# Banded attention: the row maxima enter the exponentials as a bias, GpSimd's queue in another order, one expert pair moved to the end

## The reference

```python
x = x + window_attention(group_norm(x))   # 8x8 windows shifted by 4, 8 heads, cosine scores + bias
t = tokens(x)
t = t + banded_attention(layer_norm(t))   # blocks of 128 tokens, 4 heads of 32 channels:
    # attn = q @ k.T * 32 ** -0.5 + band_mask   (0 where 0 <= i - j <= 32, else -inf)
    # out  = softmax(attn) @ v @ Wproj + bproj
t = t + moe(layer_norm(t))                # gate, top 2 of 8 experts, each 128 -> 256 (gelu) -> 128
```

## Time and profile before

| | us |
|---|---|
| median of 3 runs (range) | 3118.3 (3107.27 to 3126.27) |
| profiled execution, its time | 3125.42 |
| profiled execution, its span | 3123.6 |
| PE busy | 2461.7 |
| DVE busy | 2008.5 |
| POOL busy | 1893.4 |
| ACT busy | 1793.8 |

### The profile page before, as it was taken

The page is one execution under the profiler, slowest core; times in us unless marked ns, Lnnn a source line. Parts: engine busy times, 40 slices in busy tenths (PEclk is TensorE's granted clock), DMA queues, the critical chain, the costliest instruction groups (busy, mean ns, idle before and its releaser), DMA issues. The chain is left out here.

```text
span 3123.6 us, 73042 instructions
## 1 busy us (share of the span) xinstructions
PE 2461.7 (79%) x26418; PEld 1739.3 (56%) x26418; DVE 2008.5 (64%) x5670; ACT 1793.8 (57%) x3432; POOL 1893.4 (61%) x1569
## 2 busy tenths in 40 slices
PE   6898888888888888888888888888888888765550
PEld 3565556666655666656556566656556566543430
DVE  3688876767766777667666677677676776652110
ACT  3666676666566665666665666656665666542220
POOL 0224455676666666666666666766666666777565
PEclk8999998998898888988888889889888889877775
DMA  2011123333233333333333333333333323333542
GB/s 75 19 32 39 43 73 72 61 76 78 57 72 69 71 74 72 63 78 63 72 70 70 71 75 61 76 67 68 69 73 71 74 56 67 78 76 74 130 87 26
DMA packets 247796, 210.79 MB, mean 67 GB/s; under 512 B 35261, under 2 KB 204361, under 8 KB 247249
## 3 DMA queue, kind: packets, MB, share of 16 engines
q0 software_dynamic: 94144, 69.54, 15.8%
q1 hardware_dynamic: 153296, 136.58, 15.5%
HBM read 119.73 MB, written 90.77 MB: 67 GB/s over the span
## 5 line engine op out<-in xcount | busy, mean ns | idle before, releaser
L1159 POOL DMA_INDIRECT out_dram<-yo,back_to x540 | 854.9, 1583 | 488.6 <-PE bank_s L627 160.6
L1142 POOL DMA_INDIRECT x_sorted<-xn_c,place_i x512 | 512.4, 1001 | 271.9 <-issue 130.5
L1135 POOL TENSOR_TENSOR s_sb_a<-s_sb_a,mx_a 128x512 f32<-128x512 f32 x256 | 266.7, 1042 | 453.9 <-DVE mx_a L1518 452.5
L1510 DVE TENSOR_TENSOR s_sb_a<-bank_s,bias_a 128x512 f32<-128x512 f32 x256 | 176.2, 688 | 323.3 <-PE bank_s L627 239.1
L754 PE MATMUL bank_m<-xe,wk_e 128*128 128x512 f32 x468 | 253.8, 675 | 38.9 <-ACT hid L1017 21.5
L1135 POOL TENSOR_TENSOR s_sb_b<-s_sb_b,mx_b 128x512 f32<-128x512 f32 x256 | 268.4, 1048 | 9.5 <-DVE mx_b L1518 9.0
L761 PE MATMUL bank_m<-wk_e,hid 128*128 128x128 f32 x1872 | 257.6, 304 | 1.7 <-ACT hid L1017 1.7
L627 PE MATMUL bank_s<-kk_a,q_a 32*64 32x128 f32 x4096 | 126.2, 301 | 165.2 <-DVE st_c L1272 51.4
L986 ACT ACTIVATE p_sb_a<-s_sb_a 128x512 f32<-128x512 f32 x256 | 160.8, 628 | 166.4 <-POOL s_sb_a L1135 166.4
L761 PEld LDWEIGHTS bank_m<-wk_e,hid 128*128 128x128 f32 x1872 | 253.9, 222 | 3.5 <-issue 3.3
L981 ACT ACTIVATE pt_sb_b<-bank_to 128x512 f32<-128x512 f32 x256 | 152.6, 596 | 162.3 <-PE bank_to L688 161.8
(11 more groups left out here) (230 smaller groups left out, 5935.0 us busy)
## 6 DMA issues: line engine op xcount, KB each, us to landing
wk_e<-in_w_experts_dram SPq DMA_DIRECT2D x127, 321.0 KB, 3.1
xs<-x_sorted SPq DMA_DIRECT2D x127, 260.0 KB, 2.8
xin<-in_x_dram SPq DMA_DIRECT2D x128, 112.0 KB
x_res<-in_x_dram SPq DMA_DIRECT2D x256, 56.0 KB
out_dram<-t SPq DMA_DIRECT2D x256, 56.0 KB
out_dram<-yo,back_to POOLq DMA_INDIRECT x540
x_sorted<-xn_c,place_i POOLq DMA_INDIRECT x512
x_res<-in_x_dram SPq DMA_DIRECT2D x256, 8.0 KB
```

Source lines behind the costliest of these rows:

```text
L1135: pool.tensor_tensor(s[:, :, :], s[:, :, :], m[:, :, None].to_broadcast(shape), ALU.subtract).then_inc(s_sub[w], 1)
L1142: pool.indirect_dma_start(out=x_sorted.ap(), out_offset=bass.IndirectOffsetOnAxis(ap=place_i[:, d % 2, TILES * choice + t:TILES * choice + ...
L1159: pool.indirect_dma_start(out=out, out_offset=bass.IndirectOffsetOnAxis(ap=back_to[:, q % IDS, j:j + 1], axis=0), in_=yo[:, q % YO, j, :], ...
L1510: tt(s_sb[0][:, :, :].rearrange("p (r h) n -> p r (h n)", h=2), scores, bias_a[:, kind, :, :].rearrange("p (r h) n -> p r (h n)", h=2), AL ...
```

## The change

It has four parts.

1. **Banded maxima.** DVE computes mask minus scores, so the tile holds the negated scores (the masked places hold +1e30), and its row reduction is a minimum, which is the negated maximum. POOL's subtraction for b is gone. ACT takes exp(-tile + minimum) head by head: four instructions of 128x128, each with its column of `mx_s[1]` as bias; they wait for the minima and not for POOL. The factor 32 ** -0.5 moves into the copies of the queries (`banded_copy`).
2. **POOL's order.** In a step it is now the a subtraction, then the scatters of the step, then the add-backs, with none of the waits for the scores or for the b output. `BACK_AT` names steps only: the first pair's eight add-backs stand at 4, 4, 4, 4, 5, 6, 7, 8, the second's at 9 (four) and 10 (four).
3. **The last pass.** `FREE_PASSES = 1`: pass 34 takes no pair, so pair 56 (batch 29, groups 111 and 112) becomes the first of the tail, which has 12 pairs and not 11.
4. **Padding.** SP issues the padding writes ahead of the third load of the tail, without waiting for the scatters, and waits for them ahead of the first load of the last batch.

```diff
+FREE_PASSES = 1
-BACK_AT = (((4, 0), (4, 1), (4, 2), (4, 3), (5, 1), (5, 2), (6, 1), (6, 2)),
-           ((9, 0), (9, 1), (9, 2), (9, 3), (10, 1), (10, 2), (10, 3), (11, 1)))
+BACK_AT = ((4, 4, 4, 4, 5, 6, 7, 8), (9, 9, 9, 9, 10, 10, 10, 10))
...
-            last = i == PASSES - 1 and n == SLOTS_PER_PASS - 1
-            if i >= pairs[u].batch + (5 if n == 0 else 4) and not last:
+            if i >= pairs[u].batch + (5 if n == 0 else 4) and i < PASSES - FREE_PASSES:
...
             for n, u in enumerate(tail):
+                if n == 2:
+                    set_pads()
                 if pairs[u].batch == IMAGES - 1 and pairs[tail[n - 1]].batch != IMAGES - 1:
-                    set_pads()
+                    sp.wait_ge(pads_set, 16 * E)
                 load_pair(sp, u)
...
             def probs(w, n):
-                act.wait_ge(s_sub[w], n + 1)
+                act.wait_ge((s_sub[0], s_max[1])[w], n + 1)
                 steps_done(act, pt_ready[w], n)
-                func(flat(p_sb[w][:, :, :]), flat(s_sb[w][:, :, :]), ACT.Exp,
-                     scale=1.0 if w == 0 else float(DB) ** -0.5).then_inc(p_ready[w], 1)
+                if w == 0:
+                    func(flat(p_sb[0][:, :, :]), flat(s_sb[0][:, :, :]), ACT.Exp).then_inc(p_ready[0], 1)
+                else:
+                    for h in range(HB):
+                        last = func(p_sb[1][:, h, :], s_sb[1][:, h, :], ACT.Exp, scale=-1.0, bias=mx_s[1][:, h:h + 1])
+                    last.then_inc(p_ready[1], 1)
...
-                if tiled(n):
-                    pool.wait_ge(s_ready[0], n + 1)
-                moves(0)
                 if tiled(n):
                     below_max(0, n)
-                if tiled(nb):
-                    below_max(1, nb)
-                moves(1)
-                moves(2)
-                steps_done(pool, o_ready[1], nb)
-                moves(3)
+                if t >= 5 and on(d):
+                    for k in range(4):
+                        scatter(d, 4 * (t - 5) + k)
+                if t == 0 and on(d - 1):
+                    for k in range(12, TOP * TILES):
+                        scatter(d - 1, k)
+...
-                    tt(s_sb[1][:, :, :], scores,
-                       const("mask_b")[:, None, :].to_broadcast([P, HB, P]), ALU.add).then_inc(s_added[1], 1)
+                    tt(s_sb[1][:, :, :], const("mask_b")[:, None, :].to_broadcast([P, HB, P]), scores,
+                       ALU.subtract).then_inc(s_added[1], 1)
...
-                dve.tensor_reduce(mx_s[w][:], s_sb[w][:, :, :], AX_X, ALU.max).then_inc(s_max[w], 1)
+                dve.tensor_reduce(mx_s[w][:], s_sb[w][:, :, :], AX_X, (ALU.max, ALU.min)[w]).then_inc(s_max[w], 1)
```

More of the change, by code:

```diff
@@ L133, in shape_constants @@
     d = n[:, None] - n[None]
-    put("mask_b", np.where((d >= 0) & (d <= RADIUS), 0.0, MASKED))
+    put("mask_b", np.where((d >= 0) & (d <= RADIUS), 0.0, -MASKED))
     r = np.arange(-(WS - 1), WS, dtype=np.float32)
@@ L482, in set_pads @@
                 sp.wait_ge(totals_kept, 1)
-                for h in range(2):
-                    sp.wait_ge(scattered[h], 16 * TILES * IMAGES)
                 for e in range(E):
@@ L490, in set_pads @@
                     sp.dma_start(rows, here).then_inc(pads_set, 16)
-                sp.wait_ge(pads_set, 16 * E)
             def spill(c, h):
@@ L971, in tokens_copy, with banded_copy @@
                 func(xt_c[:, half(h)], S[2], ACT.Copy).then_inc(ln_c, 1)
-            def banded_copy(b, h, dst, src, made, kept, reader):
+            def banded_copy(b, h, dst, src, made, kept, reader, scale=1.0):
                 need_half(act, made, b, h, 1, 1)
                 need(act, reader, b - 1, TILES, 4 if h else 8)
-                func(dst[:, half(h)], src, ACT.Copy).then_inc(kept, 1)
+                func(dst[:, half(h)], src, ACT.Copy, scale=scale).then_inc(kept, 1)
             def probs_copy(w, n):
@@ L1068, in step @@
                 if t == 7 and on(b):
-                    banded_copy(b, 0, q_b, S[1], bq_ready, bq_sb, s_ready[1])
+                    banded_copy(b, 0, q_b, S[1], bq_ready, bq_sb, s_ready[1], float(DB) ** -0.5)
                 if t == 0 and on(d):
@@ L1079, in step @@
                 if t == 2 and on(b):
-                    banded_copy(b, 1, q_b, S[2], bq_ready, bq_sb, s_ready[1])
+                    banded_copy(b, 1, q_b, S[2], bq_ready, bq_sb, s_ready[1], float(DB) ** -0.5)
                 if t == 2 and on(a):
@@ L1165, in step @@
                 n, nb = TILES * i + t, TILES * i + t - LAG
[L1166 to L1172, removed]
-                                    if when == (t + TILES * (i - j), k):
-                                        add_back(u, m)
-                    if t >= 5 and on(d):
-                        scatter(d, 4 * (t - 5) + k)
-                    if t == 0 and on(d - 1):
-                        scatter(d - 1, 12 + k)
-                if tiled(n):
-                    pool.wait_ge(s_ready[0], n + 1)
-                moves(0)
                 if tiled(n):
                     below_max(0, n)
-                if tiled(nb):
-                    below_max(1, nb)
-                moves(1)
-                moves(2)
-                steps_done(pool, o_ready[1], nb)
-                moves(3)
+                if t >= 5 and on(d):
[4 more added lines that the diff above has]
+                        scatter(d - 1, k)
+                for j in (i - 1, i):
+                    for slot in range(SLOTS_PER_PASS):
+                        u = slots[j][slot] if 0 <= j < PASSES else None
+                        if u is not None:
+                            for m, when in enumerate(BACK_AT[slot][0:SUB * len(pairs[u].members)]):
+                                if when == t + TILES * (i - j):
+                                    add_back(u, m)
             for i in range(-1, PASSES):
```

## The result

The changed kernel takes 3151.19 us (median of 4 runs, 3141.21 to 3158.28) against 3116.59 us (4 runs) of the kernel before: a ratio of 1.0108, with an interval of 1.0066 to 1.0150. It is slower, by about 34 us or 1.1%. The forecast was 3107 us.

What follows compares the result with a forecast made beforehand. No engine was full (PE busy 79%); chains passing between engines set the time. From the median 3118.3 us, +11 in the full passes and -22 at the end gave 3107 us, range 3079 to 3147.

Steps and rivals of the forecast that it cites:

- The exponentials: ACT's b tile: four 128x128 pieces with bias instead of one 128x512, 0.61 us more in each of 256 tiles.
- the waits behind them: PE's waits for ACT's a copy at steps 0 and 3, to grow from 0.93 to about 1.5 us.
- The sum: Full passes: 0.61 + 0.61 + 0.13 - 0.9 = +0.45 us each, +11 us in 25; with -22 after them, -11.
- rival B: Steps 0 and 3: longer waits put PE at half clock in every pass, +35 us, 3142 us; chance 0.24.
- The forecast's own sign for this: Full passes: the forecast counts as wrong if their granted clock moves by 0.02.
- Steps 6 and 7: PE's waits there shrink: -1.4 us in one kind of pass, -0.35 in the other, mean -0.9 us a pass.
- DVE's lateness: Step 6: DVE's landing wait and 2.02 us copy shrink, DVE over 2 us earlier, step 7's scores no longer wait.
- rival C: Step 7: PE's gap shrinks and the slow stretch behind it in every second pass goes, -19 us, 3088; chance 0.20.
- The end: Last passes and tail: -10 us from an earlier tail start, -12 from add-backs covering loads, together -22 us.
- the stall: Tail, groups 113 to 115: 12.69 us of waiting for late results, to be covered by 39 us of add-backs.
- rival E: Last passes: the end gives nothing, as DVE's and PE's chain is as long as POOL's list, 3129; chance 0.07.
- D: All four pieces held behind the value copies, or dearer issues: +1.2 us a pass, +30 us, 3137; chance 0.07.

Runs made afterwards that it cites:

- e1_bias_only: The kernel before with part 1 alone (maxima as bias, no POOL subtraction for b): 3160.28 us, ratio 1.0129 to the kernel before.
- e5_filler: The changed kernel with four unused 128x128 matmuls on PE ahead of the b transpose in steps 3 and 0: 3022.73 us, ratio 0.9687 to the kernel before.
- e3_order_and_end: The changed kernel without part 1 (POOL subtracts for b again, one exponential of 128x512): 3047.10 us, ratio 0.9762 to the kernel before.
- e4_copy_first: The changed kernel with ACT's a copy moved ahead of the inverse sums in steps 2 and 7: 3018.55 us, ratio 0.9678 to the kernel before.
- e8_one_bias_copy_first: The changed kernel with one minimum and bias per row, and the a copy ahead of the inverse sums in steps 2 and 7: 2992.87 us, ratio 0.9594.

## Why the prediction was wrong

**The exponentials** were priced right: +0.61 us a tile forecast, 0.65 measured. So were the waits behind them ("about 1.5 us"; 1.51 and 1.57 as means).

**What stands behind a longer wait** was the step that failed. The sum took the two waits at their length, 1.2 us a pass, "at the same clock", and set the clock aside as rival B with a chance of 0.24. Rival B is what happened, at the two places that it named. Before, the product behind the wait had taken 3.74 us in one pass and 5.13 in the other; after, it is slow in every pass. Its price was near, 1.4 us a pass against some 1.7 for the two products (0.7 in step 0, 1.0 in step 3, as means). Its reason, "depending on how long PE stood just ahead", is not borne out as it stands: before, the wait in step 3 was 0.93 us ahead of the slow product (5.37 us) and ahead of the fast one. By steps, the full passes changed by +1.4 (step 0), +1.75 (step 3), +0.3 (steps 4 and 5), -2.3 (step 6) and +0.5 (step 7): +1.7 in all, where the sum had +0.45. e1_bias_only and e5_filler show the cause, the second without touching ACT. The forecast's own sign for this, a granted clock that moves by 0.02, did not show (0.87 and 0.89 for 0.87 and 0.90), because steps 6 and 7 gave back 3.3 us of half clock while steps 0 and 3 took 5.

**Steps 6 and 7** gave back more than the sum had: 1.8 us a pass together for 0.9. DVE's lateness went as forecast, in both kinds of pass, and with it the half clock that stood behind PE's 2.54 us wait in step 7 (2.2 us a pass before, 0 after). This is rival C, which the forecast priced at 0.75 us a pass, and it came true together with B; the forecast had them as alternatives. The next in line at step 7 was ACT, with PE's new wait of 1.55 us there, as the sum had it. The forecast reckoned with both parts together for this; e1_bias_only and e3_order_and_end show that either alone takes most of the wait away (the scores of step 7 wait 1.99 us in the mean before, 0.49 and 0.56 in these two, 0.19 in the changed kernel).

**The end** was forecast at -22 and measured at -9.3. From the last full pass to the tail it took 9 us more than forecast: three waits for landing and results that I had at 2.9 us of idle time took 4.55, 6.32 and 7.29, 9.5 us more. The tail itself, with two more groups and without the stall, cost 10.5 us and not 7.5. Two of the three waits are for DVE's results, so rival E, "DVE's and PE's own chain in the last passes is as long as POOL's list", came true in part.

**D** (pieces held behind the value copies) didn't happen: they stand 0.30 us apart there too.

What stays open is what makes the same wait harmless in one place and dear in another: 0.93 us ahead of a product of 3.74 us and of one of 5.37 in the two kinds of pass before, 0.86 us ahead of a fast one in step 0 and in 11 of 24 passes of a slow one in step 3 (e4_copy_first). It depends on more than the last wait, and no run here took it apart.

## What to carry to other kernels

Here the same product took two different times in one trace before the change, and a longer wait ahead of it made it slow in all passes. Where a trace shows this, cost such a change at the slow time in all passes too, not at the wait's own length alone. Test such a suspicion with matmuls whose result nobody uses, put into the wait: they tell clock from chain, and here they served as the remedy too. And before an instruction is made longer on the engine that PE waits for, look whether something that nobody needs soon stands ahead of what PE needs; moving the copy ahead of it gave 133 us here, where the change had cost 34.

## What was not expected of the hardware

PE's waits cost more than their length here. Filling 1.16 us of a wait of 1.4 to 1.6 us at two places took 5.1 us off a pass of 90.4 (e5_filler), and in step 4 a filler that ran past its wait, itself at the slow pace (3.65 us for eight matmuls, of which four took 1.16 us in e5_filler), still shortened a pass by 4.4 us (85.0 to 80.6). The waits at which the clock fell are short: 0.86 us ahead of the slow products in step 3 of e4_copy_first, 2.81 us in step 4 of e8_one_bias_copy_first. The Trainium skill ("TensorE: Matmul & The Clock Gate", HAM oscillation — how this bites in real kernels) describes such an oscillation of the clock in a kernel that waits 3 to 5 us for a transfer between groups of matmuls. The Trainium skill's next section on that page (A second HAM failure mode: psum-queue depth-cycling) has another kernel, in which PE idles briefly between groups and the clock falls and rises as well. This case's trace is like the second: no wait of PE in the changed kernel's full passes is over 2.9 us.
